# A four-layer conv/attention network on one core: bias and relu of every third piece of the MLP's inner layer done by ScalarE instead of VectorE

## What is computed

```python
t = t + attn(ln(t))
t = t + ffn(ln(t))

def ffn(x):                         # q_mul: to 5 exponent and 2 mantissa bits; q_acc: to float16
    h = relu(q_acc(q_acc(q_mul(x) @ q_mul(W1).T) + q_mul(b1)))     # 96 -> 384 channels
    return q_acc(q_acc(q_mul(h) @ q_mul(W2).T) + q_mul(b2))        # 384 -> 96 channels
```

## Time and profile before

| | us |
|---|---|
| runs | 4153.86, 4156.21, 4151.60 (median 4153.86) |
| profiled execution: its own time | 4153.76 |
| its span, first to last instruction | 4152.0 |
| busy in the span: PE, DVE, ACT, POOL | 3542.9, 3424.4, 2398.3, 2838.0 |
| bias and relu L1615, 192 of them | 104.1 busy |
| casts L1609, 192 of them | 84.4 busy |
| copies L1477, 192 of them | 109.0 busy |

### The profile page before, as it was taken

One profiled execution on the slowest core, in us unless ns is written; L12 is line 12 of the kernel. 1 busy time (PEld: TensorE's weight loads), 2 busy tenths in 40 slices (PEclk: granted clock), 3 DMA queues, 4 the chain that ended last, 5 costly groups with the idle time before them and its releaser, 6 DMA issues. The chain is left out here.

```text
span 4152.0 us, 38656 instructions
## 1 busy us (share of the span) xinstructions
PE 3542.9 (85%) x10080; PEld 1452.8 (35%) x10080; DVE 3424.4 (82%) x4323; ACT 2398.3 (58%) x4121; POOL 2838.0 (68%) x2328
## 2 busy tenths in 40 slices
PE   6899999999999999999999999998843878686776
PEld 2333333333333333333333333333311336364563
DVE  3999999999999999999999999999971006767676
ACT  5666766766667766666667766666522222425335
POOL 4988889999998889999988899999840000302113
PEclk8999999999999999999999999999976988676565
DMA  2555555555565555555555555555568785100001
GB/s 85 168 160 167 163 156 164 168 157 159 169 170 162 163 157 165 156 157 153 170 160 160 156 155 165 153 154 158 158 165 212 235 231 127 31 16 16 16 1 31
DMA packets 296514, 588.63 MB, mean 142 GB/s; under 512 B 82743, under 2 KB 151994, under 8 KB 295142
## 3 DMA queue, kind: packets, MB, share of 16 engines
q1 hardware_dynamic: 229222, 516.93, 43.0%
q10 hardware_dynamic: 67072, 69.23, 6.5%
HBM read 532.16 MB, written 58.28 MB: 142 GB/s over the span
## 5 line engine op out<-in xcount | busy, mean ns | idle before, releaser
L796 POOL TENSOR_TENSOR prod<-states,c_rows 128x512 f32<-128x512 f32 x1536 | 1927.8, 1282 | 179.1 <-DVE states L726 145.8
L726 DVE TENSOR_TENSOR_SCAN states<-decay,carry,bpsum 128x512 f32<-128x512 f32 x1344 | 1676.9, 1259 | 0.0
L455 PE MATMUL ypsum<-prod,identity 128*128 128x512 f32 x3072 | 1595.1, 602 | 0.5 <-POOL prod L796 0.3
L561 ACT ACTIVATE decay<-delta,decay_rate 128x512 f32<-128x512 f32 x1344 | 934.8, 711 | 313.0 <-DVE states L726 308.6
L706 DVE TENSOR_TENSOR bpsum<-bpsum,dx 128x512 f32<-128x512 f32 x1344 | 904.4, 673 | 138.7 <-PE bpsum L448 124.4
L455 PEld LDWEIGHTS ypsum<-prod,identity 128*128 128x128 f32 x3072 | 583.8, 194 | 422.8 <-issue 281.7
L448 PE MATMUL bpsum<-b_rows,select 96*128 96x512 bf16 x1344 | 522.3, 389 | 210.5 <-DVE states L726 208.0
L1655 POOL TENSOR_TENSOR y<-y,b 128x384 f16<-128x384 f16 x64 | 65.8, 1027 | 912.2 <-ACT y L1465 912.2
L448 PEld LDWEIGHTS bpsum<-b_rows,select 96*128 96x128 bf16 x1344 | 129.4, 96 | 973.3 <-DVE states L726 689.9
L561 ACT ACTIVATE bpsum<-delta,decay_rate 128x512 f32<-128x512 f32 x192 | 132.6, 691 | 309.6 <-DVE states L726 308.7
L495 PE MATMUL mm<-h_norm,w_xs 96*128 96x512 f32 x512 | 262.7, 599 | 6.0 <-ACT h_norm L627 6.0
(11 more groups left out here) (190 smaller groups left out, 4569.1 us busy)
## 6 DMA issues: line engine op xcount, KB each, us to landing
c_rows<-bc_map SPq DMA_DIRECT2D x512, 512.0 KB, 3.8
c_rows<-bc_map SPq DMA_DIRECT2D x512, 256.0 KB, 4.1
b_wide<-bc_map ACTq DMA_DIRECT2D x128, 256.0 KB, 4.6
image<-normed_map SPq DMA_DIRECT2D x192, 96.1 KB
depthwise_map<-dw_sums ACTq DMA_DIRECT2D x96, 192.0 KB, 4.3
dw_parts<-depthwise_map SPq DMA_DIRECT2D x16, 1152.0 KB, 13.2
b_wide<-bc_map ACTq DMA_DIRECT2D x128, 128.0 KB, 4.3
normed_map<-padded SPq DMA_DIRECT2D x8, 1155.0 KB, 12.4
```

Source lines behind the costliest of these rows:

```text
L455: pe.matmul(ypsum[:, group % Y_BANKS, :], identity[:, :], prod[:, n % P_RING, :], start=s == 0, stop=s == STATES - 1).then_inc(summed, 1)
L561: act.activation(into, delta[k % 2][:, g, :], ACT.Exp, scale=decay_rate[:, ORDER[k][0], g, s:s + 1]).then_inc(done, 1)
L726: dve.tensor_tensor_scan(states[:, n % H_RING, :], by, add, carry[:, at, u:u + 1], ALU.mult, ALU.add).then_inc(scanned, 1)
L796: pool.tensor_tensor(prod[:, n % P_RING, :], states[:, n % H_RING, :], c_rows[:, n // C_STATES % C_RING, n % C_STATES, :], ALU.mult).then_ ...
```

## The change

ScalarE does bias and relu of piece 2 of each chunk, one activation in place, behind its copy of that piece. It waits first on `m_taken` for its own copy to have landed. VectorE does pieces 0 and 1 only, and all three casts. The cast of piece 2 waits on a new semaphore `last_relu`; `hid_relu` now counts two per chunk. There are 64 chunks in all (8 phases of 8), so 64 instructions move. Nothing else changes.

```diff
 # ScalarE, in mlp(p), behind the three copies of a chunk and ahead of add_up(c - 1)
+                        act.wait_ge(m_taken, i + 1)
+                        act.activation(hid16[:, i % 4, :], hid16[:, i % 4, :], ACT.Relu,
+                                       bias=b1[:, phase_of(p)[1], THIRDS - 1:THIRDS]).then_inc(last_relu, 1)
 # VectorE, in to_fp8(c, k)
-                        dve.wait_ge(hid_relu, i + 1)
+                        if k == THIRDS - 1:
+                            dve.wait_ge(last_relu, CHUNKS * n + c + 1)
+                        else:
+                            dve.wait_ge(hid_relu, 2 * (CHUNKS * n + c) + k + 1)
 # VectorE, in mlp(p)
-                        for k in range(THIRDS):
+                        for k in range(THIRDS - 1):
 ...
                             if k > 0:
                                 to_fp8(c, k - 1)
+                        to_fp8(c, THIRDS - 2)
                         to_fp8(c, THIRDS - 1)
```

More of the change, by code:

```diff
@@ L1205, in batch_phase @@
                  "t_full", "t_taken", "m_full", "m_taken", "dve_step", "ln_centered", "ln_squared", "ln_var", "ln_root", "ln_ready",
-                 "gram_full", "gram_step", "small_mm", "hid_relu", "hid8_ready", "y_biased", "t_step",
+                 "gram_full", "gram_step", "small_mm", "hid_relu", "last_relu", "hid8_ready", "y_biased", "t_step",
                  "out0_stored", "out1_stored"]
@@ L1210, in batch_phase @@
          t_full, t_taken, m_full, m_taken, dve_step, ln_centered, ln_squared, ln_var, ln_root, ln_ready,
-         gram_full, gram_step, small_mm, hid_relu, hid8_ready, y_biased, t_step, out0_stored, out1_stored) = handles
+         gram_full, gram_step, small_mm, hid_relu, last_relu, hid8_ready, y_biased, t_step, out0_stored, out1_stored) = handles
         group_loaded = (group0_loaded, group1_loaded, group2_loaded, group3_loaded)
```

## The result

The change is a gain: 4132.16 us, median of 6 runs (4125.52 to 4133.31), against 4153.05, median of 6 runs of the kernel before (4150.12 to 4158.16). The profiled execution took 4132.19 us (span 4130.4).

The account below looks back on a forecast made before the run. The prediction took a ring through VectorE, TensorE, ScalarE and GpSimd's adds to bound each chunk. Gains of 4.8 (phases 10, 11, 14) and 1.6 (2, 3, 6, 7) less 0.7 (15) made 5.7 us: 4148.1, range 4138 to 4155.

Parts of the forecast that it names:

- Chunk 7: Layer-norm phases' last chunk: the second cast is held for GpSimd's bias add as the third relu was; 0.07 us gained.
- the sum of 5.7: Whole kernel, us gained: 4.8 in phases 10, 11, 14, plus 1.6 in 2, 3, 6, 7, less 0.7 in 15.
- a rival at 0.20: Chunk 7, seven phases: the cast wins the race against the bias add; 6.3 us more, 4141.8; chance 0.20.
- The ring: A chunk runs from last cast through TensorE's `mlp_out`, ScalarE's copy, GpSimd's two adds, back to VectorE's remaining relus and casts.
- The first rival: All 64 chunks: VectorE alone counts, 0.26 us back in each; 16.6 us, 4137.2; chance 0.12.
- Chunks 0 to 6: Layer-norm phases, gain at the end of chunk 6's last cast: 0.30 us in 2, 3, 6, 7; 1.54 in 10, 11, 14.
- c3 to c4 gains nothing and loses 0.08: Chunks 3 to 4: `mlp_out` does not wait for the last cast, and the new Relu starts copy L1465 0.08 us later.
- Such a slip: Chunk 2: L1545 getting in ahead of the second add, named as a wrong sign; up to 0.3 us more for c3's ring.
- ScalarE's cost: ScalarE's queue: a Relu of 0.70 us, 0.77 a chunk with wait and lost overlap, 49 us in all, partly hidden.
- The fourth rival: ScalarE: turns between Relu and Sqrt bring 56 table loads of 1.283 us, 72 us, 4226; chance 0.02.
- Phase 15: Phase without layer norm: ScalarE's queue needs 3.28 us a chunk for 3.19, 0.09 more for seven chunks; 0.7 lost.
- The range: Forecast's limits for the whole kernel: 4138 to 4155 us, meant to include the won race and part of VectorE alone.

Follow-up runs that it names:

- only_c7: Against the kernel before: only chunk 7 of each MLP phase has its third bias-and-relu on ScalarE; 4139.26 us, ratio 0.9969.
- order_c7: Kernel before, nothing moved to ScalarE; in chunk 7 only, VectorE's third bias-and-relu goes ahead of the first cast; 4140.68 us, ratio 0.9976.
- not_c7: Against the kernel before: chunks 0 to 6 have the third bias-and-relu on ScalarE, chunk 7 keeps it on VectorE; 4141.50 us, ratio 0.9980.
- act_longer: Changed kernel with one more 64-column activation on ScalarE behind each Relu; 4128.25 us, ratio 0.9942 to the kernel before.
- imm_c7: Kernel before, order unchanged; chunk 7's third bias-and-relu takes a constant instead of the bias column; 4139.78 us, ratio 0.9974.
- reorder: Kernel before, nothing moved to ScalarE; in every chunk VectorE's third bias-and-relu goes ahead of the first cast; 4143.27 us, ratio 0.9984.
- split_c7: Changed kernel, but in chunk 7 the layer norm's last reciprocal stands between first and second cast; 4138.47 us, ratio 0.9973 to the kernel before.
- alt_c7: Changed kernel, but chunk 7 runs relu 0, cast 0, relu 1, cast 1, cast 2 on VectorE; 4142.53 us, ratio 0.9977 to the kernel before.

## Why the prediction was wrong, step by step

- **Chunk 7 (the step that failed).** "Without it the second cast stands in the same place at the same time. I take it to lose the race in the same way: 0.07 gained." The place and the time were right to 0.01 us. The outcome was not, in any of seven phases: the cast went first, and 1.68 was gained instead of 0.07, 11.8 us in all for 0.6 in the sum. Of the 14.4 us that the sum of 5.7 lacks against 20.1, 11.2 are here and 3.6 in chunks 0 to 6, and phase 15 takes 0.4 back. I had it as a rival at 0.20, with the wrong price, 0.9: I let an add in ahead of the last cast, where all three casts pass unbroken and neither add is waited for. "It fell the same way in each phase seen" was no argument, since in each of them the loser was a relu with a bias column. only_c7 has this gain whole, and order_c7 has 1.42 of the 1.68 without ScalarE.
- **The ring.** Right. Without the bias add the two kernels' phases are 37 and 29 us shorter in all, though VectorE is busy for 38.4 of 41 us. The first rival (VectorE alone, 16.6 us) came nearest to the time, by luck: only_c7 and not_c7 show that the gain is not spread as it says.
- **Chunks 0 to 6.** Right in kind, too low. Forecast up to E of chunk 6: 0.30 in each of four phases, 1.54 in each of three, 5.8 us; measured 0.43, 0.75, 0.76 and 0.78, and 2.06, 2.57 and 2.08, 9.4 us. In phase 10 E of chunk 1 gained 1.47 for my 0.74: there too the bias add (3899.99) came into a run of casts (3899.48, 1.09 for three) and waited. The losses that I had worked out for chunks 0 and 1 of phase 3, 0.16 and 0.65, were 0.15 and 0.59.
- **"c3 to c4 gains nothing and loses 0.08."** Wrong in sign: that step takes 5.31 instead of 5.63 in phase 10. The layer norm's small `tensor_scalar` of chunk 3 now comes ahead of the second add and takes 0.17 us (3914.66), where it was held for 0.9. Such a slip I had named for chunk 2, where in phase 10 it did not happen.
- **ScalarE's cost.** The Relu took 722 ns for my 0.70, with 0.63 from its start to the next instruction's; the copy of the third piece is followed by it at 0.63. My 0.77 a chunk was too much: in phase 15, where ScalarE has no idle time between these instructions, a chunk grew from 2.51 to 3.17, by 0.66. The 0.77 doesn't follow from its terms either: 0.70 + 0.03 + 0.09 are 0.82, and the earlier trace rows show no overlap, since 0.60 and 0.58 are the 1.18 between the starts. In phase 15 before, a copy of 0.60 is followed at 0.51, so the 0.09 itself was right. The weight of ScalarE's queue was overrated too (act_longer). The Trainium skill's "ScalarE: Activation LUTs", in its section on what a table load costs, gives 280 + 0.833 N ns with a bias pointer. That makes an estimate of 706 ns for 512 columns; the trace has 722. Its statement that relu is in every table set agrees with the trace: `batch_phase` has no load beside L1080. The fourth rival is out. The Trainium skill's rule to keep relu on VectorE is broken here with a gain; yet order_c7, which keeps it, has 7.7 of the 20.1 us.
- **Phase 15.** 1.1 lost for my 0.7, and not as I had it. ScalarE paces it at 3.17 us a chunk (3.28 forecast), no more than the 3.19 before, and up to chunk 6 nothing is lost (21.58 for 21.69). The loss is in chunk 7, 3.04 for 1.79: the kernel before alternates between long and short chunks there and ends on a short one. As the runs show, the sign of this term is not certain.
- **The range.** It should have taken the race at its full price: two sides 0.01 us apart, seven times, are no small term.

## What to carry to other kernels

Where GpSimd and VectorE work on SBUF at once, look for operations of VectorE that are much longer than their minimum: here they were waiting, and the adds that they waited for were on the path though GpSimd was busy for only 14.5 of 41 us. Keep operations that need no column operand and no result of their neighbour together at the point where GpSimd's work arrives, and put the small ones behind them. Try the order before moving work to another engine. And where a profile shows two engines reaching for the same thing within hundredths of a us, price both outcomes, in every place where it repeats.

## What the runs showed of the hardware

The section on the chip has the engines meet only at semaphores; VectorE and GpSimd also hold each other up, in both directions. In chunk 7, at a tie of 0.01 us, the form of VectorE's next instruction decided who went first. A `tensor_scalar` with a bias column (before, not_c7) waited for the GpSimd add; a cast (after, only_c7) and a `tensor_scalar` with constants (imm_c7) did not, and a run of casts was not broken even by an add that started 0.06 us behind the first of them (reorder). The Trainium skill's "SBUF — State Buffer", in the section on who interferes with whom, has the loser blocked for the whole instruction and says that issue order, not the operation's shape, decides. The trace agrees with the first part: 1.00 and 1.05 us for relus of 0.34. For the second, the runs add that operations issued at the same time are not equal, and that a run of casts mostly passes as one. Constants alone don't save an operation: the layer norm's small L1545 has two constants, needs the result of the operation ahead of it, and was held for 0.90 us by an add that started 0.04 us ahead.

Why is open. That the column is fetched ahead of the operation, and that the add slips in meanwhile, would fit imm_c7; no run shows the fetch itself. Nor is the run of casts always safe: in chunk 2 of phase 10 after, the add got in behind the first cast, 0.10 us after its start. VectorE's and GpSimd's timelines there:

```profile
3903.80 2.52 DVE L1615 CAST hid<-hid 128x512 fp8e5<-128x512 f16 x3
```
```profile
3903.90 1.09 POOL L1662 TENSOR_TENSOR y<-y,b 128x384 f16<-128x384 f16 x1 [1.56 <-ACT y L1465]
3905.07 0.97 POOL L1665 TENSOR_TENSOR t<-t,y 128x384 f32<-128x384 f32 x1
```

In the same chunk of phase 11 it came 0.32 behind and waited, and E was 10.38 instead of 11.82.

The traces show one thing that goes with the outcome, though no run varied it by itself: how long the next cast's input had been ready. Here the relu whose result the second cast needs ended 0.02 us before the add started; in reorder it had ended 0.24 us before. Take every add in the seven layer-norm phases of the 13 traces that starts during one cast of a run, not itself held, and before the next (without chunk 7 of split_c7, where the reciprocal stands between them). In 42 cases that relu ended at most 0.02 us before the add started, or after it, and the add went first; in 76 cases it ended 0.20 us or more before, and the add waited. Nothing lies between. This fits alt_c7 as well. Phase 15 is an exception that stays open: there the add went first in seven cases with 0.20 to 0.72 us. And once a first add had held up a cast, the second add, which starts some 0.08 us behind the first one's end, held up the next cast in all 30 cases. So a race that is lost with two operations still to come costs two adds, as in chunk 7 before.
